# Quantised rows and quantised W turned by DMA transposes instead of TensorE

## What is computed

```python
h = s4d_kernel(log_dt, x, B, inv_A_real, A_imag, 1024)        # (32, 128, 1024)
h = concat([broadcast(cls_tok), h], axis=1)                   # (32, 129, 1024)
h = h + attention(layernorm(h), Wq, Wk, Wv, Wo)               # 32 heads, 8 kv heads, causal, rope
h = h + ffn(layernorm(h), w, b)

def ffn(x, w, b):
    w_q = fake_quant_per_channel(w)     # round(w / s_w), clipped to -128..127, times s_w; s_w = max|row| / 127
    x_q = fake_quant_per_token(x)       # the same per row of x
    return einsum('bsi,oi->bso', x_q, w_q) + b
```

## Time and profile before

| | |
|---|---|
| median of 3 runs | 1544.98 us |
| profiled execution, its own time | 1544.6 us |
| its span (first to last instruction) | 1542.8 us |
| granted TensorE clock, mean | 0.974 |
| TensorE busy (matmuls) | 1460.8 us, 95% |
| VectorE busy | 1298.8 us, 84% |
| ScalarE busy | 769.7 us, 50% |
| GpSimd busy | 816.2 us, 53% |
| transposes of quantised rows, line 1744 | 264 matmuls, 20.9 us busy |
| transposes of quantised W, line 1093 | 64 matmuls, 4.4 us busy |
| copies of turned rows on ScalarE, line 1788 | 33, 33.4 us busy |

### The profile page before, as it was taken

One profiled execution on the slowest core, in us unless ns is written; L12 is line 12 of the kernel. 1 busy time (PEld: TensorE's weight loads), 2 busy tenths in 40 slices (PEclk: granted clock), 3 DMA queues, 4 the chain that ended last, 5 costly groups with the idle time before them and its releaser, 6 DMA issues. The chain is left out here.

```text
span 1542.8 us, 34424 instructions
## 1 busy us (share of the span) xinstructions
PE 1460.8 (95%) x10754; PEld 1136.9 (74%) x10786; DVE 1298.8 (84%) x2344; ACT 769.7 (50%) x2710; POOL 816.2 (53%) x794
## 2 busy tenths in 40 slices
PE   5899899899999999999999999769999999999997
PEld 3899887677777777777777777556777777777774
DVE  7788587889999899999999998658988888888885
ACT  5887456666767667676676766541111111111110
POOL 2886136576766767667676676323333333333332
PEclk7999999899999999999999999879999999999998
DMA  9356525667777677677777776863333232323321
GB/s 232 97 137 154 165 93 130 178 193 208 195 202 208 197 206 198 201 206 201 207 196 200 211 196 170 277 173 125 111 113 109 95 122 82 122 99 105 116 75 48
DMA packets 220106, 244.90 MB, mean 159 GB/s; under 512 B 30001, under 2 KB 158130, under 8 KB 220050
## 3 DMA queue, kind: packets, MB, share of 16 engines
q1 hardware_dynamic: 213250, 223.14, 50.6%
q10 hardware_dynamic: 6800, 21.04, 4.5%
HBM read 138.29 MB, written 106.57 MB: 159 GB/s over the span
## 5 line engine op out<-in xcount | busy, mean ns | idle before, releaser
L1193 ACT ACTIVATE pr<-sm,ml 128x128 f32<-128x128 f32 x1024 | 398.9, 392 | 163.6 <-DVE ml L1374 163.6
L949 POOL TENSOR_TENSOR pr<-pr,ri 128x512 f32<-128x512 f32 x256 | 266.8, 1042 | 229.8 <-DVE ri L1381 223.8
L1044 PE MATMUL att_ps<-w_lo,xT_hi 128*128 128x512 f32 x792 | 326.5, 412 | 0.0
L1044 PE MATMUL att_ps<-w_hi,xT_hi 128*128 128x512 f32 x792 | 318.9, 403 | 0.0
L1044 PE MATMUL att_ps<-w_hi,xT_lo 128*128 128x512 f32 x792 | 313.4, 396 | 0.0
L1662 PE MATMUL ffn_o<-wo_hi,cT_hi 128*128 128x512 f32 x528 | 215.9, 409 | 4.0 <-ACT wo_hi L1692 2.8
L1365 DVE TENSOR_TENSOR sm<-att_ps,cst 128x512 f32<-128x512 f32 x256 | 169.9, 664 | 54.4 <-PE att_ps L1105 54.4
L1662 PE MATMUL ffn_o<-wo_hi,cT_lo 128*128 128x512 f32 x528 | 206.8, 392 | 0.0
L1662 PE MATMUL ffn_o<-wo_lo,cT_hi 128*128 128x512 f32 x528 | 205.9, 390 | 0.0
L1358 DVE STREAM_TRANSPOSE pB<-pr 128x512 f32<-128x512 f32 x256 | 176.1, 688 | 26.7 <-DMA p_blocks<-pB 24.7
L1193 ACT ACTIVATION_READ_ACCUMULATOR pr<-sm,ml 128x1 f32 x1024 | 193.2, 189 | 0.0
(11 more groups left out here) (207 smaller groups left out, 2396.3 us busy)
## 6 DMA issues: line engine op xcount, KB each, us to landing
pT<-p_blocks SPq DMA_DIRECT2D x256, 256.0 KB, 2.9
p_blocks<-pB SPq DMA_DIRECT2D x512, 64.0 KB, 2.0
h_rows<-ho SPq DMA_DIRECT2D x64, 256.0 KB, 4.0
ctx_turned<-ctxo SPq DMA_DIRECT2D x64, 256.0 KB, 3.3
h_in<-h_rows SPq DMA_DIRECT2D x32, 512.0 KB, 4.3
out_dram<-yo SPq DMA_DIRECT2D x32, 512.0 KB, 2.7
ctx_in<-ctx_turned SPq DMA_DIRECT2D x30, 512.0 KB, 3.5
hbuf<-h_rows ACTq DMA_DIRECT2D x29, 512.0 KB, 4.7
```

The lines of the kernel that those rows point to most:

```text
L949: G.tensor_tensor(pr[:, g % 4], pr[:, g % 4], ri[:, g % 2, :].unsqueeze(2).to_broadcast([P, GQ, P]), ALU.mult).then_inc(p_ready, 1)
L1044: mm = nc.tensor.matmul(bank[:], x_part[:, t[1], e, tok:tok + P], w_part[blk][:, e, :], start=(r == 0), stop=(r == EC * 3 - 1))
L1193: a = nc.scalar.activation(pr[:, g % 4, q, :], sm[:, g % 2, q, :], ACT.Exp, bias=ml[:, b[1], 0, h:h + 1], accum_out=ml[:, b[1], 1, h:h + 1])
```

## The change

All transposes of bf16 blocks leave TensorE. In their place SP issues one transposing DMA (`transpose=True`) from SBUF to SBUF for each 128 x 1024 block, on the same queue as its other DMAs:
- W: SP's body of attention tile 0 has `turn_w(0)` to `turn_w(5)` between the loads of W, each behind a wait for its `quantised`; tile 1 has the last two. `quantise_w(u)` waits for the landed transpose of block u-2 (`w_turned[u % 2]`); VectorE waits for all of them before its first write to `pB` (which lies over `wq`), TensorE before the FFN.
- Rows: SP's `body(t)` of the FFN now waits, behind `load_ctx(t+2)`, for `xq_ready` of tile t-1 and for the dense layer of tile t-3; then come `load_h(t+1)`, the transpose of tile t-1, and `store(t-2)`. `dense_layer` waits for the landed transpose, as does the next writer of the `xq` buffer. TensorE's two projection halves are issued without anything between them.
- Gone: `turn_xq` and `turn_w` on TensorE, `store_w` and the copy of line 1788 on ScalarE, the PSUM bank `ffn_xq`'s use, and the waits of `scores` and `weigh` for `w_stored`.

```diff
@@ attention, sync @@
+        def turn_w(u):
+            sp.wait_ge(quantised, u + 1)
+            sp.dma_start(wq8[:, :, u * P:(u + 1) * P], wq[:, u % 2, :], transpose=True).then_inc(w_turned[u % 2], 16)
...
             if at(t, 0):
+                turn_w(0)
+                turn_w(1)
                 load_w_pair(2)
+                turn_w(2)
+                turn_w(3)
                 load_w_pair(3)
+                turn_w(4)
+                turn_w(5)
                 no_later_keys()
             if at(t, 1):
+                turn_w(6)
+                turn_w(7)
@@ attention, tensor: turn_w and the waits for w_stored removed @@
-            if at(b, 0) and half == 0:
-                pe.wait_ge(w_stored, 6)
...
-                for u in w_turns_at(t, s):
-                    turn_w(u)
@@ attention, scalar @@
-            at_least(act, w_turned, u - 1)
+            at_least(act, w_turned[u % 2], 16 * (u // 2))
...
-                for u in w_turns_at(t, s):
-                    store_w(u)
@@ attention, vector @@
-                v.wait_ge(w_turned, EC)
+                for i in range(2):
+                    v.wait_ge(w_turned[i], 8 * EC)
@@ ffn, sync @@
+        def turn_xq(c):
+            sp.dma_start(xqT[:, c[1]], xq[:, c[1], :], transpose=True).then_inc(xq_turned[c[1]], 16)
+
         def body(t):
             if exists(shifted(t, 2), NT):
                 load_ctx(sp, shifted(t, 2))
+            c = shifted(t, -1)
+            if exists(c, NT):
+                sp.wait_ge(xq_ready, number(c) + 1)
+                if not fixed(c) or number(c) >= 2:
+                    sp.wait_ge(dense, 2 * number(c) - 2)
             if exists(shifted(t, 1), NT) and not at(t, 0):
                 load_h(sp, shifted(t, 1))
+            if exists(c, NT):
+                turn_xq(c)
             if exists(shifted(t, -2), NT):
                 store(shifted(t, -2))
@@ ffn, tensor @@
-                pe.wait_ge(xq_stored, u + 1)
+                pe.wait_ge(xq_turned[c[1]], TURN_COUNT * (c[0] + 1))
...
-                project(pe, t, 0, PER_HALF)
-            if exists(c, NT) and not at(t, 1):
-                turn_xq(c)
-            if exists(t, NT) and not at(t, 0):
-                project(pe, t, PER_HALF, 2 * PER_HALF)
-            if at(t, 1):
-                turn_xq(c)
+                project(pe, t, 0, 2 * PER_HALF)
...
+        for i in range(2):
+            pe.wait_ge(shared["w_turned"][i], 8 * EC)
@@ ffn, scalar @@
-            if exists(c, NT):
-                act.wait_ge(xq_turned, number(c) + 1)
-
-                nc.scalar.copy(xqT[:, c[1], :, :].rearrange("p c k -> p (c k)"), psb[:]).then_inc(xq_stored, 1)
@@ ffn, vector @@
-            at_least(v, xq_turned, u - 1)
+            if not fixed(t) or u >= 2:
+                v.wait_ge(xq_turned[t[1]], TURN_COUNT * t[0])
```

More of the change, by code:

```diff
@@ L710, in attention_stage @@
     quantised = sem("quantised")
-    w_turned = sem("w_turned")
-    w_stored = sem("w_stored")
+    w_turned = shared["w_turned"]
     scales_out = shared["scales_out"]
@@ L784, in w_quantise_at @@
         return ()
-    def w_turns_at(t, s):
-        if at(t, 0):
-            return {1: (0, 1), 3: (2, 3), 6: (4, 5)}.get(s, ())
-        if at(t, 1):
-            return {0: (6,), 2: (7,)}.get(s, ())
-        return ()
     def wo_rounds_at(t, s):
@@ L797, in wo_rounds_at @@
         return (2 * (s + n) - 2, 2 * (s + n) - 1) if at(t, NB) and s > 0 or at(t, NB + 1) and s == 0 else None
-    def w_bank(u):
-        return S_BANK[u % 4] if u < 6 else C_BANK
     def iterations(eng, body):
@@ L1078, in turn_x @@
             mm.then_inc(x_turned, 1)
[L1080 to L1094, removed]
         def scores(b, half):
@@ L1110, in weigh @@
             u = number(b)
-            if at(b, 0) and half == 0:
-                pe.wait_ge(w_stored, EC)
             pe.wait_ge(p_whole[half], 64 * (u + 1))
@@ L1471, in ffn_stage @@
     PER_HALF = 3 * EC
+    TURN_COUNT = 16
     def sem(name):
@@ L1488, in ffn_stage @@
     O_BANK = [psum["ffn_o0"], psum["ffn_o1"]]
-    psb = psum["ffn_xq"]
     wo_turned = sem("wo_turned")
@@ L1513, in ffn_stage @@
     xq_ready = sem("xq_ready")
-    xq_turned = sem("xq_turned")
-    xq_stored = sem("xq_stored")
+    xq_turned = [sem(f"xq_turned{i}") for i in range(2)]
     dense = sem("dense")
@@ L1737, in turn_c_end @@
             mm.then_inc(c_end_turned, 1)
[L1739 to L1745, removed]
         def dense_layer(c, half):
@@ L1981, in program @@
         shared["ctx_stored"] = [sem(f"ctx_stored{i}") for i in range(2)]
+        shared["w_turned"] = [sem(f"w_turned{i}") for i in range(2)]
         shared["p_parted"] = [sem(f"p_parted{i}") for i in range(2)]
```

## The result

The changed kernel takes 1539.44 us, the median of nine runs (1536.61 to 1541.97), against 1544.98 before: a ratio of 0.9963, 95% interval 0.9951 to 0.9974. It is 0.4% faster where 1557.9 us and slower was forecast, and within 1 us of the first rival, 1538.8. The time does lie in the stated range of 1532 to 1680, but the forecast named the wrong direction. The closeness to the rival is partly luck, as the part on the forecast shows.

What follows compares the result with a forecast made beforehand. TensorE, busy 95% of the span, was taken as the bound; 1544.6 - 3 (W in attention) + 14 (tile 3) + 0 (steady FFN) + 2.3 (end) = 1557.9 us, range 1532 to 1680.

Steps and rivals of the forecast that it cites:

- the first rival: Whole kernel: cheap transposes landing just within the budget, steady FFN gain 13.8 us, sum 1538.8 us; chance 0.25.
- The transposes' worth on TensorE: Steady FFN iteration: eight transposes and the switch cost 0.51 us, so the period falls from 14.94 to 14.43.
- The budget and its half: FFN loop: 5.85 us from xq ready to landed transpose; half of any excess is added to each period.
- X: FFN loop: real time from xq ready to landed transpose, taken as 6.9 us.
- both rows that I set as its bounds: Cost per DMA packet in two profile windows: 0.030 us for many small pieces, 0.174 us for 4 KB ones.
- The load ahead: SP's queue in the FFN loop: h load issued just before the transpose, whose data queue behind it; lands in 4.3 us.
- The lower bound of 5.8: FFN loop: transpose as cheap as any 256 KB DMA, 1.4 us of data, giving 5.8 us from xq to landing.
- the 27 steady periods: Steady FFN loop: forecast worth nothing, 27 periods at +0.0 us.
- Tile 3: FFN start: transpose behind SP's context wait and loads; dense layer 11.5 us late, 3 from tile 0, plus 2.5 clock: +14.0.
- The 2.5 of clock: Dense layer of tile 3: matmuls run 2.5 us longer because idle time lowers TensorE's clock.
- Tile 0 and the end: FFN's first dense layer starts 2.2 us later, after some 4.5 us of idle; the last one +2.3 us.
- W in the attention stage: Attention stage: TensorE saves 4.1 us over eight W blocks, less ScalarE and load delays; -3 taken, ends -4 and +2.

Runs made afterwards that it cites:

- the runs with two and three transposes: Changed kernel with one or two extra row transposes a tile into spare buffers, the dense layer waiting for all: 1550.89 us and 1571.15 us.
- the rows alone: Kernel before the change with only the quantised rows turned by DMA, W still by TensorE: 1540.19 us, ratio 0.9971.

## Why the forecast missed

**The transposes' worth on TensorE: right.** 0.51 us was read from the distance of starts and 0.56 to 0.57 came off the period. VectorE did cover it: it still waits 0.70 to 0.79 us for its second residual.

**The budget and its half: right.** 5.85 us was worked out. It is 5.5 to 5.6, since TensorE's next piece starts 0.2 us before the first one on record, and the runs with two and three transposes show the period growing by half of the excess over that.

**X: mis-sized, and this turned the direction.** The step that failed is "X = 0.1 (SP waking) + 4.3 + the transpose's own data", with 2.5 us for the data: 6.9. In the iteration shown it is 0.2 until SP issues the load, 3.7 until that lands at 1212.56, and 1.0 more until the transpose lands at 1213.56: 4.9, which is below the budget where 6.9 was above it. Two terms are too large.
- The data is cheaper. The share of the 16 engines rose from 50.6% of 1542.8 us to 55.1% of 1537.8:

```profile
q1 hardware_dynamic: 213250, 223.14, 50.6%
```

```profile
q1 hardware_dynamic: 256546, 233.89, 55.1%
```

The first row is of before, the second of after. The difference is 1067 engine-microseconds for 41 transposes, 1.6 us on each engine for one, counting also what other transfers were slowed. The last row transpose has the queue for itself (queue view of 1524.20 to 1527.40):

```profile
q1 hardware_dynamic: 1056, 0.26, 42.6%
```

That is 1.4 us on each engine, 0.021 us a packet. That the piece is 256 B fits (43,296 more packets under 512 B, 1056 a transpose), its price of 0.04 did not. It lies below both rows that I set as its bounds.
- The load ahead was charged in full, and then all of the data. The load lands in 3.7 now (below, the page's DMA issues: count, KB each, median us to landing), and the transpose, issued 0.39 behind it, 1.0 us after it, less than the 1.4 that its data takes alone: the two overlap. The last row transpose, with no load ahead, lands 3.07 after its issue, so the load ahead costs 0.4 of issue and 1.2 of landing. No run has the load behind the transpose. The lower bound of 5.8 rests on the same adding-up and was itself 0.9 too high.

```profile
h_in<-h_rows SPq DMA_DIRECT2D x32, 512.0 KB, 3.7
```

So the 27 steady periods gave 15.1 us where 0 stood in the sum, and where 13.8 stood in the first rival's.

**Tile 3: right in mechanism, near in size.** +14.0 was forecast, 3 of it handed on from tile 0. Measured +9.1 of lateness, 0.9 of which the kernel brought from the attention stage, and 1.6 of slower matmuls. What was too much is mostly the 3 us handed on: SP's h load there is only 0.9 late (1105.75 against 1104.86), and from its issue to the dense layer it is 6.5 us where 6.8 stood. The 2.5 of clock compared sixteen matmuls (5.95) with fifteen recorded ones (3.40); sixteen take 3.62, so the row of before gives 2.3. What such an idle time costs differs: 1.6 here, but in the trace of the rows alone, behind 9.88 us of idle, the sixteen take 6.42 us, 2.8 more.

**Tile 0 and the end: right, small.** Dense layer 0 starts at 1058.28, 1.2 late, but 0.9 of that came from the attention stage and only 0.3 is the transpose's, where 2.2 stood. The idle time before it is 2.19 us, and the clock did not fall (1.00 from 1058.28 to 1061.30). The last dense layer starts 3.14 us after its xq (1524.20 to 1527.34) instead of 2.2, +0.9 where +2.3 was forecast.

**W in the attention stage: wrong.** -3 was forecast, and no gain can be measured. TensorE was busy 40 of 40 us there, and that was taken for a path to the end. Its work was taken off and its waits grew by as much: 2.5 us of lead were there at tile 0 and were gone by tile 6.

With the measured sizes the sum is 1544.6 + 9.1 + 1.6 - 15.7 = 1539.6; the 0.9 of the seam before the FFN is inside the 9.1, and the end's 0.9 inside the 15.7. That the first rival came within 1 us is partly luck. It had the cheap X right, but its -4.1 for W was 5.0 us off in this execution (+0.9 at the seam), against 1.1 too much at tiles 0 to 3 (10.9, measured 9.8 without the seam) and 3.1 too little gain from there to the end (12.6 net, measured 15.7).

## What to carry to other kernels

A DMA that replaces work on a busy engine is worth that work only if it lands inside a budget; work out the budget from the trace first, and do not add the full landing time of a transfer ahead of it in the queue, since much of that is latency that overlaps. Then walk the issuing queue from its first to its last iteration: a single wait for something unrelated in one of 33 iterations took back 11.6 of the 17 us by the medians (9.4 of 15 by the ratios) that the change is worth without it, and moving it cost nothing that could be measured. And a busy engine is not yet the path: in the attention stage the work taken off TensorE came back as waiting. Use one large transposing DMA rather than several small ones.

## What the runs showed of the hardware

A transposing DMA holds SP's queue for 1.24 us whether it turns 128 x 128 or 128 x 1024 bf16, where a plain one holds it for 0.33. Right behind another large one it can be more: of three of 1024 columns in a row the second took 1.76. Alone, a 256 KB transpose lands 3.0 us after its issue; the last of eight of 32 KB lands in 2.3. The Trainium skill (VectorE: DVE Perf Modes, "The three transpose paths") gives 1309 ns for one 128x128 block by DMA; the 1.27 us from one such DMA to the next is near it, the 2.3 us to landing is not, and 1024 columns cost no more to issue, so it must not be multiplied by blocks. Its 261 GB/s for a transposing DMA (DMA: Bandwidth & Descriptors, "Latency and other measured facts") would be 1.0 us for 256 KB; the 1.4 us on each engine of the last transpose is 192 GB/s, less than stated, and still small enough to hide.
